# A graph kernel's order of work: VectorE's pieces one per tile, row matmuls from tile 4, dst sums between main matmuls

## What is computed

```
diff  = (x[dst] - x[src]) / dx                      # per edge, 16 channels
d1    = segment_sum(diff, dst) - segment_sum(diff, src)
S     = segment_sum(slope, dst)
x     = layernorm(x + (x - dt * (x * d1 + g * S)))
x     = layernorm(x + segment_sum(edge_attr_16, dst) / count(dst))
```

## Time and profile before

| | before |
|---|---|
| median of 3 runs | 4688.31 us |
| the profiled execution's own time | 4681.29 us |
| its span, first to last instruction | 4679.5 us |
| TensorE busy | 4485.3 us, 96% |
| VectorE busy | 3823.7 us, 82% |
| GpSimd busy | 3597.0 us, 77% |
| ScalarE busy | 1430.6 us, 31% |
| mean granted TensorE clock | 0.996 |

### The profile page before, as it was taken

One profiled execution on the slowest core, in us unless ns is written; L12 is line 12 of the kernel. 1 busy time (PEld: TensorE's weight loads), 2 busy tenths in 40 slices (PEclk: granted clock), 3 DMA queues, 4 the chain that ended last, 5 costly groups with the idle time before them and its releaser, 6 DMA issues. The chain is left out here.

```text
span 4679.5 us, 90558 instructions
## 1 busy us (share of the span) xinstructions
PE 4485.3 (96%) x31379; PEld 2683.7 (57%) x31380; DVE 3823.7 (82%) x8582; ACT 1430.6 (31%) x1014; POOL 3597.0 (77%) x3133
## 2 busy tenths in 40 slices
PE   3999999999999999999999999999999999999996
PEld 2666555555555555555555555555555555555554
DVE  6888888878888788888888888887888878888886
ACT  4332233222332223322332223322332223322220
POOL 7777777777777777777777777777777777777770
PEclk9999999999999999999999999999999999999998
DMA  3111111111111111111111111111111111111110
GB/s 91 34 34 43 34 33 34 40 37 34 33 34 41 36 34 33 34 43 34 34 34 34 43 34 34 33 42 34 34 34 34 43 34 34 34 34 42 34 22 7
DMA packets 212186, 168.11 MB, mean 36 GB/s; under 512 B 126538, under 2 KB 195662, under 8 KB 211912
## 3 DMA queue, kind: packets, MB, share of 16 engines
q1 hardware_dynamic: 111734, 139.99, 9.3%
q0 software_dynamic: 100000, 25.80, 6.2%
q10 hardware_dynamic: 428, 2.01, 0.1%
HBM read 164.74 MB, written 2.81 MB: 36 GB/s over the span
## 5 line engine op out<-in xcount | busy, mean ns | idle before, releaser
L584 PE MATMUL ps_src<-hi_hot,spread 128*128 128x391 bf16 x25000 | 4309.4, 329 | 91.4 <-DVE hi_hot L858 91.3
L379 POOL DMA_INDIRECT x_src<-in_x_dram,src_i x3125 | 3592.0, 1149 | 955.9 <-issue 861.2
L584 PEld LDWEIGHTS ps_src<-hi_hot,spread 128*128 128x128 f16 x25000 | 2185.7, 97 | 1659.1 <-DVE hi_hot L858 199.4
L858 DVE TENSOR_SCALAR hi_hot<-col_h,hi_f,scale 128x1564 bf16<-128x1564 f16 x3125 | 2127.4, 697 | 205.9 <-PE ps_src L584 205.8
L790 DVE TENSOR_TENSOR spread<-lo_rows,halves 128x640 f16<-128x640 f16 x1250 | 554.4, 485 | 82.1 <-issue 80.0
L525 PE MATMUL ps_x<-xwin,node_of_dst 128*128 128x48 bf16 x3125 | 575.0, 187 | 11.5 <-ACT node_of_dst L467 11.5
L442 ACT CAST parts<-pay 128x425 bf16<-128x425 f32 x125 | 72.5, 580 | 1642.5 <-DVE pay L750 1642.5
L525 PEld LDWEIGHTS ps_x<-xwin,node_of_dst 128*128 128x128 bf16 x3125 | 298.9, 97 | 228.7 <-issue 12.2
L457 ACT CAST parts<-left 128x400 bf16<-128x400 f32 x125 | 71.6, 573 | 1041.2 <-DVE left L847 1041.2
L465 ACT ACTIVATE node_of_dst<-rel_all,row_neg 128x3200 bf16<-128x3200 f16 x125 | 369.8, 2959 | 6.6 <-DMA rel_all<-rel_d 6.6
L467 ACT ACTIVATE node_of_dst<-node_of_dst,ones 128x3200 bf16<-128x3200 bf16 x125 | 370.3, 2963 | 4.1
(11 more groups left out here) (110 smaller groups left out, 1006.1 us busy)
## 6 DMA issues: line engine op xcount, KB each, us to landing
rel_all<-rel_d SPq DMA_DIRECT2D x125, 800.0 KB
x_src<-in_x_dram,src_i POOLq DMA_INDIRECT x3125
a<-in_edge_attr_dram SPq DMA_DIRECT2D x125, 200.0 KB
a<-in_edge_attr_dram SPq DMA_DIRECT2D x125, 25.0 KB, 1.8
src_i<-in_src_dram SPq DMA_DIRECT2D x125, 12.5 KB, 1.6
dst_i<-in_dst_dram SPq DMA_DIRECT2D x125, 12.5 KB, 1.7
xwin<-xparts_d SPq DMA_DIRECT2D x125, 12.0 KB, 1.7
dst_sum<-in_dst_dram SPq DMA_DIRECT2D x1, 1562.5 KB
```

What stands on the lines that cost most here:

```text
L379: nc.gpsimd.indirect_dma_start(x_src[:, b, j * F:(j + 1) * F], None, x[:, :], bass.IndirectOffsetOnAxis(ap=src_i[:, b, j:j + 1], axis=0)). ...
L584: last = nc.tensor.matmul(ps_src[:, q, 0:HB], spread[:, b, j, k, :, :].rearrange("p l f -> p (l f)"), hi_hot[:, slot(b, j), q * HB:(q + 1) ...
L858: v.tensor_scalar(hi_hot[:, slot(b, j), :], col_h[:, :], hi_f[:, b, j:j + 1], scale[:, b, j:j + 1], ALU.is_equal, ALU.mult).then_inc(hi_ho ...
```

## The change

The table `PIECES` is rewritten: the ten `spread` pieces stand one per tile in tiles 12 to 21 instead of two per tile in 8 to 12; `dst_rel` and the five `dst_hot` stand in tiles 1 to 5 instead of 13 to 16, and what was in tiles 1 to 6 (`diff` to `parts`) moves to tiles 5 to 10; `slope`, `window`, `attr_left` and `attr_parts` move to tiles 22 to 24. The row matmuls go from tiles 8 to 20 to tiles 4 to 16. The 25 dst sums, one block behind tile 7 before, are put one behind each pair of main matmuls from tile 9 to the first pair of tile 15, with their waits ahead of tile 9. No instruction is added or removed, and GpSimd's, ScalarE's and SyncE's programs are the same.

```diff
-        SUM_AT, ROWS_AT = 7, 8
-        PIECES = {0: ["x_of_dst"], 1: ["diff"], 2: ["pay"], 3: ["scale"], 4: ["scaled"], 5: ["left"], 6: ["parts"],
...
+        SUM_AT, ROWS_AT = 9, 4
+        PIECES = {0: ["x_of_dst"], 1: ["dst_rel", "dst_hot"], 2: ["dst_hot"], 3: ["dst_hot"], 4: ["dst_hot"], 5: ["dst_hot", "diff"],
...
             def tile(c, b, j, stop, sums_of=None, rows_of=None):
...
+                    s = (j - SUM_AT) * 4 + q
+                    if sums_of is not None and 0 <= s < J:
+                        one = take_sum(dst_of_node[:, sums_of, :, :], s)
+                        if s == J - 1:
+                            one.then_inc(win_sum_ready, 1)
...
                 for j in range(J):
+                    if j == SUM_AT and finish:
+                        pe.wait_ge(dst_hot_ready, c + 2)
+                        pe.wait_ge(parts_ready, c + 2)
+                        pe.wait_ge(win_added, c + 1)
                     if j == ROWS_AT and begin:
...
-                    tile(c, b, j, not finish and j == J - 1, b if begin else None)
-                    if j == SUM_AT and finish:
-                        window_sums(c + 1, 1 - b, span)
+                    tile(c, b, j, not finish and j == J - 1, 1 - b if finish else None, b if begin else None)
+                    if j == SUM_AT + (J - 1) // 4 and finish:
+                        further_sums(span)
```

More of the change, by code:

```diff
@@ L256, in gnn_kernel @@
         TROW, TCOL = TAIL // P, TAIL % P
-        SUM_AT, ROWS_AT = 7, 8
-        PIECES = {0: ["x_of_dst"], 1: ["diff"], 2: ["pay"], 3: ["scale"], 4: ["scaled"], 5: ["left"], 6: ["parts"],
-                  8: ["spread"] * 2, 9: ["spread"] * 2, 10: ["spread"] * 2, 11: ["spread"] * 2, 12: ["spread"] * 2,
-                  13: ["dst_rel"], 14: ["dst_hot"] * 2, 15: ["dst_hot"] * 2, 16: ["dst_hot", "slope"], 17: ["window"], 19: ["attr_left"], 21: ["attr_parts"]}
+        SUM_AT, ROWS_AT = 9, 4
+        PIECES = {0: ["x_of_dst"], 1: ["dst_rel", "dst_hot"], 2: ["dst_hot"], 3: ["dst_hot"], 4: ["dst_hot"], 5: ["dst_hot", "diff"],
+                  6: ["pay"], 7: ["scale"], 8: ["scaled"], 9: ["left"], 10: ["parts"],
+                  12: ["spread"], 13: ["spread"], 14: ["spread"], 15: ["spread"], 16: ["spread"], 17: ["spread"], 18: ["spread"],
+                  19: ["spread"], 20: ["spread"], 21: ["spread"], 22: ["slope"], 23: ["window", "attr_left"], 24: ["attr_parts"]}
         FIRST_HALF = ["dst_rel", "dst_hot", "slope", "attr_left", "attr_parts"]
@@ L570, in window_sums, with further_sums @@
                 sums(dst_of_node[:, b, :, :]).then_inc(win_sum_ready, 1)
+                further_sums(span)
+            def further_sums(span):
                 def more(g, first):
@@ L576, in window_sums, with tile @@
                 further_in(pe, span, more)
-            def tile(c, b, j, stop, rows_of=None):
+            def tile(c, b, j, stop, sums_of=None, rows_of=None):
                 if j % HOTS_READY == 0:
```

## The result

The changed kernel took 4560.94 us (median of 5 runs, 4560.26 to 4561.38) against 4688.31 before (4681.98 to 4691.01): ratio 0.9726, 95% interval 0.9713 to 0.9740. I had forecast 4915 us. What came true is the rival *Faster*, TensorE sets the pace, for which 4571 us had been worked out.

The account below looks back on a forecast made before the run. GpSimd's gathers (36.35 us a chunk) were taken to bound the kernel, ahead of TensorE's 35.39. 4679.5 + 231.8 - 5.3 = 4906.0 us of span, plus 1.8 and 7.0, gave 4915 us; range of 8 in 10: 4780 to 5040.

Parts of the forecast that it names:

- Faster: Rival: gathers held below 4.2 us a chunk, so TensorE sets the pace; 4571 us, chance 11%.
- What bounds the kernel: In the loop, TensorE's line at 35.39 us a stage and GpSimd's at 36.4 run side by side; the slower counts.
- Why a gather takes what it takes: Gathers beside VectorE: let in where the last two-input operation ends, needing 0.82 us more; 5.1 us a chunk held.
- The step that failed: Single spreads: VectorE's cycle becomes 1.00 us, gathers are held 0.75 us instead of 0.15; at most +2.85 us a chunk.
- a reason for a wrong sign: Caveat on the slowdown: if two-input operations don't hold gathers, the sign of the term is off.
- `dst_hot`: Gathers beside `dst_hot`: two and a half held 0.75 us, 1.9 together instead of 1.2; at most +0.7 us a chunk.
- `attr_left`: `attr_left` and `window` together in tile 23: the gather of 1.48 us there mostly spared, -0.5 us a chunk.
- Sum: Gather hold in all: 3.55 - 1.15 - 0.5 = +1.9 us a chunk, +231.8 us over 122 chunks.
- TensorE's sums: Dst sums between main matmuls: 0.056 us each, no change taken, from a span of -0.7 to +1.4 us a stage.
- The later deadline: VectorE needs the last gather behind tile 5's one-hot instead of tile 1's: -5.3 us once per kernel.
- 1.25 misses every other one: Argument against Faster: doors open every 1.00 us in 15 tiles, and a gather asking at 1.25 us misses every other.

Follow-up runs that it names:

- 24 gathers: Kernel before, but from chunk 3 on GpSimd gathers 24 of each chunk's 25 tiles: 4562.65 us, ratio 0.9732 (chip A); 0.9934 on chip D.
- spreads in pairs: Changed kernel with its ten spreads two behind each one-hot again, in tiles 12 to 16: 4590.06 us, ratio 0.9794 (chip A).
- pieces alone: Kernel before with the changed kernel's `PIECES` table, TensorE's program as before: 4590.98 us, ratio 0.9794 (chip A); 1.0141 on chip E.
- single spreads: Kernel before with spreads one per tile in tiles 8 to 17, the other pieces behind them: ratio 1.0531 (chip B), 1.0209 (chip C).

## Why the prediction was wrong

- **What bounds the kernel** was right. GpSimd's line at 36.35, TensorE's at 35.39: the table shows it in five kernels, and 24 gathers show it by itself.
- **Why a gather takes what it takes** was right as a rule for the rows of before and wrong where it was carried on. "It isn't let in between a one-hot and the two-input operation behind it" is what happens to a gather that begins in a certain part of the one-hot (the 2.40 us one began 0.58 us before its end; the 1.67 us one above 0.45). Ahead of a spread, one that begins later is let in there or isn't held at all, and one that begins with the one-hot mostly isn't held either.
- **The step that failed** is "the gather asks at 1.25, into the next one-hot, and gets in at 2.00. It is held 0.75 us instead of 0.15 ... at most +2.85 us a chunk". In the changed kernel none of 1,272 gathers beside spreads was held so. It treated VectorE's cycle as a fixed 1.00 us that gathers have to fit, and gathers alone as what can be held. Instead a gather that comes late in the one-hot holds the next one-hot for 0.2 us, the cycle becomes 1.25 us, GpSimd's own pitch, and the fit repeats itself. The sign stood in the trace of before: three one-hots in a row take 2.06 us in the earlier trace rows, where one with no gather beside it takes 0.68 or 0.69 and three in the kernel with spreads in pairs (at 2053.40) take 1.89, and the one at 2025.80 of before takes 0.88. I had read the earlier trace rows for the gather's time alone. Measured for spreads: held time 0.86 us a chunk before and 0.31 after, so -0.5 instead of the top's +2.85. It is luck of the entry as much as a rule: with another entry the hold there rose, to 1.13 and 1.59. What I had named as a reason for a wrong sign, that two-input operations don't hold gathers, was not it: they do.
- **`dst_hot`**, +0.7 at most: the hold itself was right here, its size and the sign of the whole were wrong. About one gather a stage is held to the end of a `dst_hot` (118 of 1.6 to 2.2 us), where I had two and a half at 0.75. In all the gathers beside it were held 1.2 us a chunk before and about 0.9 after, so -0.3.
- **`attr_left`**, -0.5: right, it measured -0.55 (0.67 us held in tiles 17 and 19 before, 0.12 in tile 22 after).
- **Sum**: +1.9 us a chunk forecast, -1.3 measured (5.14 to 3.86), of which the stage could use only 36.35 - 35.37 = 0.98, since TensorE's line comes then. 122 x 0.98 = 120 of the 121 us of span. The threshold given for this rival (hold below 4.2 us a chunk) was right: 3.86 passed it, 4.42 with spreads in pairs did not.
- **TensorE's sums** at 0.056 us and no change: right, 35.37 against 35.39 us a stage on a quiet TensorE.
- **The later deadline**, -5.3 us: it has no meaning once gathers are ahead; nothing shows it.
- **The weight of the rival.** "1.25 misses every other one" was given as the reason against it. It is no argument while VectorE has slack (82% busy), since then it can be VectorE that moves.

## What to carry to other kernels

When two engines share something and one of them has slack, don't compute the fit of the one against a fixed cycle of the other: ask who is held when the gather comes first, whether the slower beat then repeats itself, and from which entries it does. A line that bounds by 1 us a stage is worth no more than that, however much its own time falls, because the next line stands right behind it. And time a change that fills TensorE on more than one chip: this one is worth -2.7% on one and +3.5% on another.

## What the runs showed of the hardware

- An indirect gather of 128 rows and VectorE's operations hold each other by order of arrival. Ahead of a single spread, a gather that begins within 0.1 us of the one-hot's end takes 0.94 to 0.95 us and mostly stretches the next one-hot from 0.68 to 0.89; one that begins 0.3 to 0.4 us before it is let in at that end; one that begins 0.4 to 0.5 us before it mostly waits for the two-input spread as well (1.67 to 1.70 us); one that begins with the one-hot mostly takes 0.94 to 0.95. Ahead of other operations the limits lie elsewhere. The Trainium skill (SBUF — State Buffer, "Who interferes with whom") says that issue order, not the shape of the operation, decides who blocks. The rows agree: gather and one-hot take 0.95 and 0.89 us in the changed kernel's spreads, and 1.70 and 0.68 in those of the pieces alone. That a two-input operation leaves a gather's issue alone, its inference quoted in the prediction, doesn't hold here: the gather of 1.67 us ends 0.82 us behind the spread.
- With the same program chips differ by up to 8.5% (4688 to 5088 us for the kernel before, at a mean granted clock of 0.99 to 1.00 on chips A, B and D and 0.98 on C and E). For the kernel before on chip D 39 us of it lie ahead of the loop (the first main matmul starts at 117.3 us, where it was 78.4). The rest is standstills of TensorE, mostly of 0.3 to 1.6 us, that no wait explains, and stretches at half clock behind them; on chip C the changed kernel has a clock of 0.943 where the kernel before has 0.98. Each chip served for one group of runs, so the record doesn't tell a chip's lasting trait from its condition at the time. Where in the stage they fall depends on the program: in the changed kernel in tiles 13 to 15, where the interleaved sums end, in the kernel before around the stage's ends (tiles 20 to 24 and 0 to 5). Their cause stays open, and so does why single spreads cost 5.3% on chip B and 2.1% on C.
